# Fetching the two chosen experts from memory, and more quads of a routed convolution computed by pairs of rows

## What is computed

```python
for t in range(3):                                   # STEPS
    attn = softmax(q . k(x))                         # two heads, over the 1024 pixels
    weights = softmax(masked(pooled(attn, x) @ Wmlp) / 1.5)
    top_vals, top_idx = top_k(weights, 2)            # two of K = 4 experts, per image
    wsel = weights on those two, normalised
    x_mod = x * (1 + attn_map * scale * a)
    y = sum over e of wsel[:, e] * conv3x3(x_mod, We[e], be[e])
    allowed = allowed without the first choice
    x = y
```

## Time and profile before

| | |
|---|---|
| median of 3 runs | 677.94 us (677.34 to 678.18) |
| profiled execution, its own time | 679.21 us |
| its span | 677.4 us |
| PE busy | 647.1 us (96%) |
| DVE busy | 552.7 us (82%) |
| ACT busy | 290.9 us (43%) |
| POOL busy | 172.4 us (25%) |
| first quad of phase 1 to first of phase 2 | from 129.95 to 194.94 us |
| quads 16 to 23 | from 321.67 to 459.08 us |
| second block | from 459.08 us to the end |

### The profile page before, as it was taken

The page is one execution under the profiler, slowest core; times in us unless marked ns, Lnnn a source line. Parts: engine busy times, 40 slices in busy tenths (PEclk is TensorE's granted clock), DMA queues, the critical chain, the costliest instruction groups (busy, mean ns, idle before and its releaser), DMA issues.

```text
span 677.4 us, 14867 instructions
## 1 busy us (share of the span) xinstructions
PE 647.1 (96%) x6176; PEld 258.9 (38%) x6176; DVE 552.7 (82%) x904; ACT 290.9 (43%) x383; POOL 172.4 (25%) x156
## 2 busy tenths in 40 slices
PE   7868999899999999999999999999999999999995
PEld 7433333333333333333333334433444444444442
DVE  5699876979987988896486697848988888888885
ACT  3753622322322322132202310043688778778761
POOL 2100320008201900370032030321334234235230
PEclk9979999899999999999999999997999999999998
DMA  9930000000000000000000000000032132132132
GB/s 331 209 64 1 2 1 1 1 1 1 3 1 1 2 1 1 1 1 2 1 1 15 1 1 1 2 9 9 10 70 48 40 71 48 40 71 48 40 71 63
DMA packets 55119, 21.76 MB, mean 32 GB/s; under 512 B 51250, under 2 KB 51988, under 8 KB 55060
## 3 DMA queue, kind: packets, MB, share of 16 engines
q1 hardware_dynamic: 54772, 20.66, 12.4%
q10 hardware_dynamic: 288, 0.21, 0.1%
HBM read 10.38 MB, written 8.39 MB: 28 GB/s over the span
## 4 chain that ended last, share of the span: by engine, by line
PE 77%; DVE 12%; issue 1%; ACT 1%; DVEq 0%; ACTq 0%
PE conv L683 35%; PE conv L738 12%; PE att L754 11%; PE att L473 5%; PE conv L649 5%; DVE xpad L1199 3%; PE att L552 3%; PE att L564 2%; PE att L725 2%; DVE stats L1302 2%; DVE comb L1288 1%; PE att L531 1%; DVE x L1257 1%; DVE x L1264 1%; DVE x L1508 1%
## 5 line engine op out<-in xcount | busy, mean ns | idle before, releaser
L683 PE MATMUL conv<-xpad,comb 64*64 64x512 f32 x2592 | 290.2, 595 | 2.8 <-DVE x L1264 2.7
L1508 DVE TENSOR_TENSOR x<-conv,x 128x512 f32<-128x512 f32 x288 | 178.0, 683 | 24.1 <-PE conv L738 22.8
L683 PEld LDWEIGHTS conv<-xpad,comb 64*64 64x64 f32 x2592 | 98.5, 134 | 170.7 <-issue 160.1
L1288 DVE SCALAR_TENSOR_TENSOR comb<-experts,wsel,comb 128x576 f32<-128x576 f32 (+1 forms) x138 | 113.5, 888 | 5.2 <-ACT comb L866 4.8
L738 PE MATMUL conv<-rstack,wse 98*128 98x512 f32 x288 | 95.7, 437 | 1.7 <-DVE xin L1297 0.9
L866 ACT ACTIVATE comb<-experts,wsel 128x576 f32<-128x576 f32 (+2 forms) x49 | 35.2, 769 | 109.2 <-PE conv L683 69.7
L754 PE MATMUL att<-x,cmp 64*32 64x512 f32 x1280 | 80.5, 601 | 0.0
L738 PEld LDWEIGHTS conv<-rstack,wse 98*128 98x128 f32 x288 | 48.5, 190 | 70.6 <-DVE x L1508 63.9
L1199 DVE SCALAR_TENSOR_TENSOR xpad<-att,x 128x1024 f32<-128x1024 f32 x46 | 54.0, 1216 | 20.6 <-PE att L531 20.4
L1645 POOL TENSOR_TENSOR x<-x,xin 128x1024 f32<-128x1024 f32 x15 | 35.9, 2396 | 111.4 <-ACT x L1008 111.4
L876 ACT ACTIVATE x<-conv,bias 128x512 f32<-128x512 f32 x40 | 25.2, 681 | 83.8 <-PE conv L683 83.8
(11 more groups left out here) (187 smaller groups left out, 604.6 us busy)
## 6 DMA issues: line engine op xcount, KB each, us to landing
x<-in_x SPq DMA_DIRECT2D x32, 256.0 KB, 5.1
out<-comb SPq DMA_DIRECT2D x30, 256.0 KB, 3.2
rstack<-rstack SPq DMA_DIRECT2D x16, 128.0 KB, 3.8
experts<-in_We SPq DMA_DIRECT2D x1, 1152.0 KB
out<-comb SPq DMA_DIRECT2D x4, 128.0 KB, 2.2
wide<-in_c_wide SPq DMA_DIRECT2D x1, 192.0 KB, 6.6
x<-in_c_sum SPq DMA_DIRECT2D x1, 160.0 KB
small<-in_c_small ACTq DMA_DIRECT2D x1, 142.5 KB, 3.8
```

The source lines that it names most:

```text
L683: last = nc.tensor.matmul(conv[own[to], h, HW * rows:HW * rows + HW], comb[own[rows], q % 2, n, tap(t)], xpad[own[rows], 2 * (q % 2) + n, ...
L1288: v.scalar_tensor_tensor(comb[:, q % 2, n, cols], experts[:, e, cols], wsel[:, p % 2, j + QP * n, e:e + 1], comb[:, q % 2, n, cols], ALU.m ...
L1508: v.tensor_tensor(img(prod[i])[:, rows, :], img(conv[:, unit, :])[:, rows, :], xip[s][:, kh + 16 * h:kh + 16 * h + 16, kw:kw + W], ALU.mul ...
```

## The change

The tables of all forms of all four experts (seven blocks of 192 columns, the minus form now made once by POOL) are written to a tensor `forms` in the chip's memory at the start. From quad 6 on, SP reads for each of the quad's four images the numbers of its two chosen experts (`top_at`) into registers and fetches just their tables into `chosen`, which lies where `experts` lay: eight transfers of 64 partitions per quad. A fetch starts when DVE has read the buffer for the quad before. ACT begins the mixture with the first choice, DVE adds the second (`combine_two`, two additions). POOL makes the numbers and their weights, `top_at` and `top_weight`, in nine more steps; for phase 1 DVE does (`pick_experts`).

Twelve quads are short: 4, 6, 8, 9, 10, 12, 13, 14, 16, 18, 20, 22. In the last two phases a short quad's result goes to `x` (for phase 5 to the spare slots 3 and 7) and one operation of 2048 columns adds it to `xin` (`add_residual`). The channel statistics of quads 16 to 21 are taken by ACT (`late_stats`). The constants of the second block are loaded later, between the fetches for quads 21 and 22, and expanded in quad 21.

```diff
-SHORT = tuple(QP * p + j for p in range(1, LAST) for j in (0, 2))
+SHORT = tuple(QP * p + j for p in range(1, PHASES) for j in range(QP - 1) if j != 1 or p in (2, 3))
...
+        top_at = packed(small, 0, 2 * GP * TOP).bitcast(mybir.dt.int32).rearrange("p (a i r) -> p a i r", a=2, r=TOP)
...
+        chosen = experts[:, :, :].rearrange("p (n r) c -> p n r c", n=2)
+        minus_forms = row_sums[:, :, :, :, :].rearrange("p a b c d -> p (a b c d)")[:, 0:K * ROW].rearrange("p (k c) -> p k c", k=K)
+        forms = nc.dram_tensor("forms", (K, C, FORM_BLOCKS * ROW), F32, kind="Internal")
...
-            first = slot(q, 0)
+            first = slot(q, 0) if q < QP * (PHASES - 1) else SPARE
...
-            return q - 1 in SHORT and q % QP == QP - 1
+            return q - 1 in SHORT and q % QP == QP - 1 and q < QP * LAST
...
+            def write_forms():
+
+                eng.wait_ge(forms_ready, 4)
+                table = forms[:, :, :].rearrange("k p c -> p k c")
+                eng.dma_start(table[:, :, 4 * ROW:7 * ROW], experts[0:C, :, 0:3 * ROW]).then_inc(forms_out, 16)
+                eng.dma_start(table[:, :, ROW:4 * ROW], experts[0:C, :, ROW:4 * ROW]).then_inc(forms_out, 16)
+                eng.dma_start(table[:, :, 0:ROW], minus_forms[0:C, :, :]).then_inc(forms_out, 16)
...
+                p, j = divmod(q, QP)
+                if j == 0 or q == GATHER_FROM:
+                    eng.wait_ge(top_ready, p)
+                return [eng.value_load(top_at[64 * m:64 * m + 1, p % 2, j + QP * n, r:r + 1], min_val=0, max_val=K - 1)
+                        for n in range(2) for m in range(2) for r in range(TOP)]
...
+            def gather(q):
+
+                at = iter(chosen_of(q))
+                first, size = (0, 4 * ROW) if q in SHORT else (4 * ROW, TAPS * C)
...
+                    else:
+                        eng.wait_ge(comb_added[n], added(q - 1))
+                    for m in range(2):
+                        for r in range(TOP):
+                            eng.dma_start(chosen[own[m], n, r, 0:size],
+                                          forms[bass.ds(next(at), 1), :, first:first + size].rearrange("k p c -> (k p) c")).then_inc(gathered[n], 16)
+
+            write_forms()
+            eng.wait_ge(forms_out, 16 * FORMS_WRITTEN)
+            for q in range(GATHER_FROM, QP * LAST + 6):
+                gather(q)
+            eng.wait_ge(residual_added, residuals(QP * LAST + 2))
             for dst, src in LATE_CONSTS:
                 eng.dma_start(dst, src).then_inc(late_consts_in, 16)
+            for q in range(QP * LAST + 6, QUADS):
+                gather(q)
...
                 if j == 0 and at == (0, 0):
                     if p == 1:
                         permute(1)
-                    attend(p + 1, "scores", sw)
-                    attend(p + 1, "values", uw)
+                    if p < PHASES - 1:
+                        attend(p + 1, "scores", sw)
+                        attend(p + 1, "values", uw)
+                elif j == 1 and at == (0, 1):
+                    logits(p + 1)
                 elif at == ((2, 0) if j == 0 else (1, 1)):
...
-                        nc.scalar.activation(comb[:, q % 2, n, cols], experts[:, 0, cols], ACT.Identity,
-                                             scale=wsel[:, p % 2, j + QP * n, 0:1]).then_inc(comb_begun[n], 1)
+                        if q >= GATHER_FROM:
+                            eng.wait_ge(gathered[n], 64 * (q - GATHER_FROM + 1))
+                            first, weight = chosen[:, n, 0, cols], top_weight[:, p % 2, j + QP * n, 0:1]
+                        else:
+                            first, weight = experts[:, 0, cols], wsel[:, p % 2, j + QP * n, 0:1]
+                        nc.scalar.activation(comb[:, q % 2, n, cols], first, ACT.Identity, scale=weight).then_inc(comb_begun[n], 1)
...
+            def late_stats(q, n):
+
+                k, before = slot(q, n), 2 * (q - QP * LAST) + n
+                if q in SHORT:
+                    eng.wait_ge(residual_added, residuals(q))
+                else:
+                    eng.wait_ge(final_emptied, final_parts(q, 1))
+                part = stats[:, k, 0, 0:1]
+                nc.scalar.activation(unused, xin[:, k, :], ACT.Copy, scale=1.0 / (32 * S), accum_out=part).then_inc(late_mean, 1)
...
-                if p == LAST:
-                    expanded_weights()
+                    if q - 2 >= QP * LAST:
+                        for n in range(2):
+                            late_stats(q - 2, n)
+                    if q == QP * (PHASES - 1) + 1:
+                        expanded_weights()
...
+                if q < GATHER_FROM:
+                    for n in range(2):
+                        eng.wait_ge(comb_added[n], added(q))
+                        v.tensor_tensor(comb[:, q % 2, n, 0:ROW], comb[:, q % 2, n, 3 * ROW:4 * ROW], comb[:, q % 2, n, 0:ROW],
+                                        ALU.subtract).then_inc(minus_ready, 1)
...
                 if hurried(q):
                     eng.wait_ge(conv_full, sections(q - 2, 1))
-                    v.tensor_scalar(comb[:, q % 2, 0, cols], experts[:, 0, cols], wsel[:, p % 2, j, 0:1], None, ALU.mult)\
+                    eng.wait_ge(gathered[0], 64 * (q - GATHER_FROM + 1))
+                    v.tensor_scalar(comb[:, q % 2, 0, cols], chosen[:, 0, 0, cols], weight(0, 0), None, ALU.mult)\
                         .then_inc(own_begun, 1)
...
+                for n in range(2):
+                    if hurried(q) and n == 0:
+                        eng.wait_ge(own_begun, hurried_upto(q))
                     else:
-                        eng.wait_ge(comb_begun[n], 2 + q + 1 - (0 if n else sum(hurried(k) for k in range(q))))
-                    v.scalar_tensor_tensor(comb[:, q % 2, n, cols], experts[:, e, cols], wsel[:, p % 2, j + QP * n, e:e + 1],
+                        eng.wait_ge(comb_begun[n], 2 + q + 1 - (0 if n else hurried_upto(q - 1)))
+                    v.scalar_tensor_tensor(comb[:, q % 2, n, cols], chosen[:, n, 1, cols], weight(n, 1),
                                            comb[:, q % 2, n, cols], ALU.mult, ALU.add).then_inc(comb_added[n], 1)
...
+            def add_residual(q):
+
+                eng.wait_ge(short_emptied, 2 * SHORT.index(q) + 2)
+                first = slot(q, 0)
+                both = xin[:, first:first + QP + 1:QP, :]
+                first = first if q < QP * (PHASES - 1) else SPARE
+                v.tensor_tensor(both, both, x[:, first:first + QP + 1:QP, :], ALU.add).then_inc(residual_added, 1)
...
+            pick_experts(1)
...
-                    if q - 1 >= QP * LAST:
-                        final(q - 1, 1)
                     if q - 1 in SHORT:
                         finish_rows(q - 1, 1)
+                    elif q - 1 >= QP * LAST:
+                        final(q - 1, 1)
...
-                        combine(q + 1)
+                        (combine_two if q + 1 >= GATHER_FROM else combine)(q + 1)
...
-                    if q >= QP * LAST:
+                    if q >= QP * LAST and q not in SHORT:
                         final(q, 0)
-                    if p == LAST and j >= 2:
-                        final_stats(QP * LAST + j - 2)
-                    if p == PHASES - 1:
-                        if j < 2:
-                            final_stats(QP * LAST + 2 + j)
-                        elif j == 2:
-                            final_stats(QP * LAST + QP)
-                        else:
-                            final_stats(q - 2)
-                            final_stats(q - 1)
+                    if q - 1 in SHORT_FINAL:
+                        add_residual(q - 1)
+                    if q == QUADS - 1:
+                        final_stats(q - 1)
...
+                eng.wait_ge(forms_ready, 3)
+                eng.wait_ge(shift_full, 1)
+                v.tensor_tensor(minus_forms[:, :, :], plus, middle, ALU.subtract).then_inc(forms_ready, 1)
...
+                v.tensor_copy(top_at[:, p % 2, :, :], cmp[:, 0, :, 0:TOP, 2]).then_inc(top_ready, 1)
...
+                v.tensor_tensor(top_weight[:, p % 2, :, :], half[:, :, :, 0], half[:, :, :, 1], ALU.add).then_inc(top_weighed, 1)
```

More of the change, by code:

```diff
@@ L112 @@
 CUT = H // 2 + 1
-SMALL = (4 + K) * D + 29
+SMALL = (4 + K) * D + 29 + K
+TOP = 2
+GATHER_FROM = QP + 2
+FORM_BLOCKS = 7
+FORMS_WRITTEN = 3
 EARLY = GP + 5
```

137 lines of the change are left out of this document (100 added, 37 removed).

## The result

| | |
|---|---|
| before, median of 7 runs | 677.94 us (677.26 to 678.18) |
| changed, median of 7 runs | 680.59 us (679.38 to 683.23) |
| ratio | 1.0047, 95% interval 1.0033 to 1.0061 |
| changed, once more beside other runs, 11 runs | 679.73 us, ratio 1.0024 (1.0015 to 1.0033) |
| profiled execution of the change, its own time and span | 683.23 us, 681.4 us |

The change makes the kernel slower by 0.2 to 0.5%, where a gain of 0.2% was forecast. The profiled execution is the slowest of its seven, 2.6 us above their median. That will matter.

A forecast was written before the change was run, and what follows sets the result against it. PE sets the pace with DVE close behind, and a short quad already ends on DVE. Terms 0.3 + 4.7 - 6.65 = -1.65 take the profiled 679.21 to 677.6; predicted median 676.3 us, range 671 to 682.

The forecast's parts named there:

- Picking the experts (+0.3): DVE, ahead of quad 4's attention reduction: seven operations of 0.2 us, of which +0.3 us show.
- Quads 16 to 23 (-6.65): Converting quads 16, 18, 20, 22 to short ones, less waits in quads 19, 21 and 23: sum -6.65 us.
- The phases' term (+4.7): Third and fourth phase, quads 9 and 13 short: row sums and finishes make PE wait, +2.3 us a phase, together +4.7.
- quad 9 lasts 15.3 us: Quad 9 as a short quad behind a short one: second pass waits for DVE's finish; 15.3 us against 16.43 full.
- The residual's addition: DVE's addition of 2048 columns in the last phases: 2.3 us, between 1.8 and 3.5.
- SP did not bound: Rival, slower: reads and issues outlast a quad from 1.35 us a read; 695 at 1.5, 785 at 2.2. Chance 0.18.
- PE kept nothing: Rival, faster: DVE's pieces overlap PE better, six conversions give up to 25 us: 653, likelier 665. Chance 0.16.
- GpSimd's chain: Rival, slower: nine operations join the routing; bias 4 us late for PE's permutation in both phases gives 684. Chance 0.08.
- PE idle before quad 9's second pass: Sign: PE idles some 2 us there, released by L1388, in a quad of about 15.3 us.
- Quad 19 ended by L1434: Sign: quad 19 lasts near 20 us and ends on L1434.
- ScalarE's first copy for quad 22: Sign: this copy ends on a transfer; such waits in every quad would mean SP bounds.
- DVE busy for 95%: Sign: in the third and fourth phase DVE has two additions per quad and is busy for about 95%.

The follow-up runs named there:

- Fetching alone: Kernel before with its short quads kept, plus two fetched experts and the last images' statistics on ScalarE: 679.95 us, ratio 1.0030; a second time 679.72 us, 1.0026.
- the version with the extra products: Against the change, PE repeats the first two taps of the first pass in quads 9, 10, 13 and 14, result thrown away: 678.24 us, ratio 1.0003.
- the two orders: Change with upper finish ahead of differences, lower final addition ahead of row sums, residual right behind the finish: 665.03 us; with quads 9, 13 full, 663.93 us.
- the residual first: Against the change, DVE adds a short quad's residual right behind its upper finish, not behind the next quad's final addition: 677.45 us, ratio 0.9979.
- the order run: Against the change, DVE's upper finish stands ahead of the next quad's differences, the lower final addition ahead of its row sums: 679.19 us, ratio 1.0017.

## Why the prediction was wrong, point by point

- **Picking the experts (+0.3) was mis-sized: 1.4 us.** I let the attention's operations cover what in truth stands ahead of them on the same engine. Fetching alone shows it, 20.68 against 19.29 us. Fetching costs another 0.4 us that the sum has not.
- **Quads 16 to 23 (-6.65) were mis-sized: -5.5** (149.57 against 155.07 us). Quad 16 19.13 us (19.15 forecast), quad 18 12.01 (11.8), quad 19 20.16 (19.9), quads 20 and 21 together 31.84 (12.5 + 18.9 = 31.4), quad 22 13.92 (12.8), quad 23 18.42 (19.4). The largest step that failed is quad 22, which gained 2.5 us and not 3.5: its second pass waits for the final addition behind the residual, and the residual took 3.65 us in place of 2.28 (last section). The two additions took 2.94 in place of 1.54, which cost nothing, since DVE waited 0.50 us for PE behind them. Quad 20's 13.92 and quad 21's 17.92 each miss by 1.0 to 1.4, in opposite directions; only their sum is set, by the fetch for quad 22.
- **The phases' term (+4.7) was right as a wait and lacked the clock behind it.** Without a fall the two stretches grow by 5.1 us (65.94 + 65.93 against 2 x 63.37): quad 8 20.4, quad 9 15.30, quad 10 14.16. With falls they grow by 5.8 + 4.3 in the profiled execution and by 2.6 + 4.3 in the second. The step that failed is "quad 9 lasts 15.3 us", "quad 10 14.0", worked out with all of PE's records at full pace. What was left out is what PE's clock does when PE itself begins to idle; the falls in quads 9, 10 and 14 of the profiled execution are worth 1.7 + 1.6 + 1.7 = 5.0 us.
- **The residual's addition** was taken at 2.3 us and measured 2.27 and 2.28 where nothing ran beside it.
- **SP.** A read takes 0.354 us in the median, with its two register instructions 0.52, and eight of them 5.3 to 5.9 us from the first read to the first issue where nothing held SP up, 0.66 to 0.73 each; I took 0.8. A transfer took 0.63 to issue (eight in 5.06). SP did not bound, and quad 22's tables landed 20.9 us after quad 20 began, as forecast. That it agrees to the tenth is luck: the constants took 3.5 us and not 4.5, the reads 5.6 and not 6.4, and the last transfer landed 4.7 us after the issues had ended and not 2.5. The Trainium skill ("DMA: Bandwidth & Descriptors", latency and other measured facts) gives a floor of about 600 ns for a tensor load; here the shortest took 267 ns. SP's rows on the change: count, then ns at least, median and at most, first and last start.

```profile
L443 SPq TENSOR_LOAD <-small x144: 267/354/714, 135.6 to 420.5; - x144
...
L458 SPq DMA_DIRECT2D experts<-forms x144: 468/469/1361, 141.4 to 425.9; - x144
```

- **The rivals.** PE kept nothing: no short quad behind a short one took 11.75. GpSimd's chain was not late: from its first operation beside quad 9 to the completed ranks it took 7.1 us (221.44 to 228.58), 10.4 before, its last product of quad 9's ranking ended at 241.8, and PE permuted at 253.33 without waiting. What made the result slower, the small operations ahead of quad 4's additions and the clock, was no rival of mine.
- **The signs to look for.** PE idle before quad 9's second pass, released by L1388: yes, 1.5 us. Quad 19 ended by L1434: yes. ScalarE's first copy for quad 22 ended by a transfer: yes. DVE busy for 95% in the third and fourth phase: only in quads 9 and 13 (14.54 of 15.30 us without a fall); quad 11, with 10.54 of 16.05, is far from it, for the additions are gone.

The balance without falls in quads 8 to 15: +1.4 + 5.1 - 5.5 = +1.0 us, where the sum of the prediction was -1.65. All three terms came out on the slow side, by 1.1, 0.4 and 1.15 us, so the forecast gain is gone before the clock comes in. The falls come on top. How much they cost in the median execution the runs tell only roughly: the change lies 5.4 to 6.2 us above the version with quads 9 and 13 full, of which the waits explain 5.1 and the clock 0.2 to 1.1; against the version with the extra products the clock is worth 1.5 to 2.4. The range of the prediction, 671 to 682, holds the measured 680.59, but it was drawn for a read's price, the residual and the waits; nothing in it stands for the pick or the clock, and that it holds is luck. What was worth having is in the two orders.

## What to carry to other kernels

Before work is taken from the engine that sets the pace, find what it will wait for, and ask what else its idle time costs: on PE two waits of 1.5 to 2.1 us in one quad sometimes brought half the clock, and with it 1.7 us more; filling the wait with idle products is a quick test. A short quad behind a full one was worth its 3.9 us (quads 16 and 18); behind another short one, where DVE has no cover left, it was worth nothing in either order. When a quad already ends on DVE, order DVE's list by who waits: what releases PE first, what only the next pass needs behind it. Here a few moved calls gave 1.5% (674.38 to 663.93), but one of the two moves alone gave almost nothing, since the residual became the new wait. And a profile is one execution: where the clock is drawn anew each time, take the sizes of a theory from two profiles and the stretches between fixed marks, and before a slow quad is charged to the total, look whether the next one gives it back.

## What the runs showed of the hardware that I had not expected

**The clock falls in some executions and not in others.** Quads 9, 10, 13 and 14 have the same waits of 1.46 to 2.11 us in each execution of the change; the granted clock fell in three of the four in one profile, in one of the four in the second, in none where only the constants were moved, and in three again with the residual first. Behind the longer wait ahead of quad 20 (3.94 us) it was lower in all six profiles that have this wait.

**VectorE and GpSimd hold each other up.** In quad 22 of the order run DVE's two additions (two inputs in SBUF) took 6.63 us in place of 1.54, while beside them GpSimd multiplied weights for the second block; in the change the same GpSimd operation met the residual:

```profile
423.33 6.89 POOL L1786 TENSOR_TENSOR x<-x,wse 98x1152 f32<-98x1152 f32 x1 [55.40 <-ACT wse L1017]
430.33 3.59 POOL L1788 TENSOR_SCALAR x<-x,masks 98x1152 f32<-98x1152 f32 x1
```

```profile
429.91 2.63 POOL L1778 TENSOR_TENSOR x<-x,wse 98x1152 f32<-98x1152 f32 x1 [53.02 <-ACT wse L1017]
432.65 5.12 POOL L1780 TENSOR_SCALAR x<-x,masks 98x1152 f32<-98x1152 f32 x1
```

The one takes 2.63 or 6.89 us and the other 5.12 or 3.59, by what DVE does beside them. The Trainium skill ("SBUF — State Buffer", who interferes with whom) says that a VectorE instruction with two SBUF inputs contends with a GpSimd one that reads SBUF; the rows agree, and show that VectorE pays too, here up to 5 us. No run separates the two, so this reading is argued and not shown.
